# A decoder layer on one core: ones row by a transfer, group weights on VectorE, single scatters, bias halves moved

## The reference, cut to what matters

```python
x = _layernorm(x + _L0_attn_ref(x, ...), axis=-1)
x = _layernorm(x + _L0_xattn_ref(x, ctx_768, ...), axis=-1)
x = _layernorm(x + _L0_ffn_ref(x, ...), axis=-1)
```

```python
mean_sq = (jnp.sum(jnp.square(re), -1) + jnp.sum(jnp.square(im), -1)) / (2.0 * H * M)
rs = jax.lax.rsqrt(mean_sq[..., None] + 1e-05)
y = re * rs * norm_scale[:H * M] @ W_re + im * rs * norm_scale[H * M:] @ W_im
return y * x_gate @ out_proj_w
```

## Time and profile before

| | |
|---|---|
| median of 3 runs | 228.33 us (228.28 to 228.69) |
| profiled execution | 228.0 us, of it span 226.2 us |
| busy: PE, PEld | 183.7 (81%), 132.8 (59%) |
| busy: DVE, ACT, POOL | 160.5 (71%), 116.8 (52%), 71.4 (32%) |
| chain that ended last | PE 63%, DVE 22%, issue 4%, DMA 4%, ACT 4% |
| TensorE's mean granted clock | 0.93 |

### The profile page before, as it was taken

How to read it: one execution, slowest core, us unless ns; L and a number is a source line. 1 busy time by engine, 2 the same in 40 slices (tenths; PEclk the granted TensorE clock), 3 DMA queues, 4 the chain that set the end, 5 groups by cost and what they waited for, 6 DMA issues and landing times.

```text
span 226.2 us, 4759 instructions
## 1 busy us (share of the span) xinstructions
PE 183.7 (81%) x1727; PEld 132.8 (59%) x1727; DVE 160.5 (71%) x394; ACT 116.8 (52%) x245; POOL 71.4 (32%) x86
## 2 busy tenths in 40 slices
PE   7769999979799888999979739832799999998700
PEld 6434556654254646657636728632799999887500
DVE  2956999988899667477459625688466787754791
ACT  2056989722565225267937424544335676551353
POOL 8950000000030000025665286673015555451000
PEclk9979999999999999999979676995899999999985
DMA  5999999992996395989196013014221110003111
GB/s 151 294 197 251 190 260 204 382 407 105 244 380 158 85 317 182 244 295 280 64 293 219 7 41 113 12 34 107 60 63 49 38 35 26 19 3 109 36 42 41
DMA packets 13465, 34.15 MB, mean 151 GB/s; under 512 B 2095, under 2 KB 5733, under 8 KB 13442
## 3 DMA queue, kind: packets, MB, share of 16 engines
q1 hardware_dynamic: 12354, 32.22, 50.4%
q0 software_dynamic: 1088, 1.62, 2.4%
HBM read 27.96 MB, written 6.38 MB: 152 GB/s over the span
## 4 chain that ended last, share of the span: by engine, by line
PE 63%; DVE 22%; issue 4%; DMA 4%; ACT 4%; another core or an unknown queue 1%; POOL 0%; DVEq 0%; SPq 0%; ACTq 0%; POOLq 0%
PE bank L776 8%; PE bank L483 8%; PE bank L559 7%; PE bank L536 7%; PE bank L759 6%; PE bank L493 5%; PE bank L502 5%; PE bank L546 5%; PE bank L471 2%; PE bank L757 2%; DVE map_e L1421 2%; DVE neg_max L1341 2%; DVE dsm L1151 2%; DVE ph L1445 2%; DMA convw_sb<-conv_w 2%
## 5 line engine op out<-in xcount | busy, mean ns | idle before, releaser
L1588 DVE SCALAR_TENSOR_TENSOR ctx_slot<-bank,ctx_slot 128x512 f16<-128x512 f32 (+1 forms) x28 | 18.7, 672 | 15.2 <-ACT ctx_slot L1070 10.4
L1807 POOL DMA_INDIRECT ret<-ctx_slot,ctxT_slot x20 | 19.8, 989 | 30.2 <-ACT ctx_slot L1083 26.8
L536 PE MATMUL bank<-ctxT_slot,w_conv 97*64 97x500 f32 x96 | 23.5, 628 | 2.4 <-ACT pc L917 1.4
L1070 ACT ACTIVATE ctx_slot<-bank 128x512 f16<-128x512 f32 (+1 forms) x28 | 16.1, 582 | 15.8 <-PE bank L759 15.8
L483 PE MATMUL bank<-xpad,w_conv 128*128 128x448 f32 x48 | 20.3, 580 | 3.2 <-DVE w_conv L1142 3.2
L776 PE MATMUL bank<-home,ctx_slot 128*112 128x128 f16 (+1 forms) x192 | 14.7, 229 | 7.1 <-ACT ctx_slot L1070 7.1
L559 PE MATMUL bank<-ctx_slot,ph 125*64 125x96 f32 (+1 forms) x384 | 19.6, 265 | 0.4 <-DVE res L1451 0.4
L559 PEld LDWEIGHTS bank<-ctx_slot,ph 125*64 125x64 f32 (+1 forms) x384 | 18.1, 146 | 2.3 <-DVE res L1451 1.1
L483 PEld LDWEIGHTS bank<-xpad,w_conv 128*128 128x128 f32 x48 | 9.8, 206 | 13.3 <-issue 9.3
L776 PEld LDWEIGHTS bank<-home,ctx_slot 128*112 128x112 f16 (+1 forms) x192 | 12.8, 122 | 7.6 <-ACT ctx_slot L1070 7.4
L1341 DVE TENSOR_REDUCE neg_max<-bank 120x1 f32<-120x1500 f32 x8 | 13.7, 1717 | 4.3 <-PE bank L536 4.2
(11 more groups left out here) (220 smaller groups left out, 448.1 us busy)
## 6 DMA issues: line engine op xcount, KB each, us to landing
ctx_slot<-ctx SPq DMA_DIRECT2D x16, 576.0 KB, 5.5
ctxT_slot<-ctx_T SPq DMA_DIRECT2D x16, 562.5 KB, 8.7
w_raw<-w SPq DMA_DIRECT2D x16, 256.0 KB, 6.9
slots<-w_raw SPq DMA_DIRECT2D x4, 910.0 KB, 30.7
ctxT_slot<-slots SPq DMA_DIRECT2D x20, 65.0 KB, 1.9
convw_sb<-conv_w SPq DMA_DIRECT2D x3, 256.0 KB, 6.0
ctxT_slot<-ret SPq DMA_DIRECT2D x3, 224.0 KB, 3.3
small_sb<-small SPq DMA_DIRECT2D x1, 546.0 KB, 10.2
```

The source lines that it names most:

```text
L536: mm = pe.matmul(bank[j * GAP:j * GAP + rows, n, 0:SN], qk_all[:, at:at + rows], ctxT_slot[:, s, j, n * SN:(n + 1) * SN], start=True, stop ...
L1070: nc.scalar.activation(hh[:, n % 3, :, 0:cols], bank[:, n % 3, :].rearrange("p (f t) -> p f t", f=FC) [:, :, 0:cols], ACT.Relu).then_inc(t ...
L1588: V.scalar_tensor_tensor(hl[:, n % 3, :, 0:cols], bank[:, n % 3, :].rearrange("p (f t) -> p f t", f=FC) [:, :, 0:cols], 0.0, hh[:, n % 3, ...
L1807: G.indirect_dma_start(ret[:], bass.IndirectOffsetOnAxis(ap=xs_u[:, t, D + 1:D + 2], axis=0), out_st[:, t % OB, :], None, bounds_check=2 * ...
```

## The change

The ones row is no longer filled by POOL: a new input `ones`, one row of 9000 numbers, is transferred into it by SP behind the tokens and ahead of the context, and PE's wait at L706 is for that transfer. `w_blk` is made by DVE in two instructions, in the middle of `phases(0, 0)` and ahead of the clip; `norm_scale`, `w_ri` and a new table `group_of` (32 columns) stand in `first` for that. `scatter` takes one pair and one choice, so it is one instruction, and POOL's list places these between its other work; `split_low(1, 4)` comes ahead of three of them, and the last two splits and three `plus_beta` wait for `m_rw7`, the last pair's route weights. `bias_low` goes from turn 5 to the last turn, behind `select(3)`. Four more fillers stand on PE: one ahead of `logits(6)`, one ahead of `turn_x2(7)`, one ahead of `logits(7)`, and one ahead of `hidden(0)`.

```diff
@@ -73,8 +73,9 @@
 V_DOWN = 20
 
 
-FIRST = [("w_in", 3 * D), ("conv_b", 3), ("theta", M), ("slope", 1), ("dist", L), ("score_scale", 1), ("deriv", 3)]
-SMALL = [("norm_scale", 2 * M), ("w_ri", 2 * M * H), ("group_mask", D), ("ident", D), ("w_out", D), ("w_qT", D),
+FIRST = [("w_in", 3 * D), ("conv_b", 3), ("theta", M), ("slope", 1), ("dist", L), ("score_scale", 1), ("deriv", 3),
+         ("norm_scale", 2 * M), ("w_ri", 2 * M * H), ("group_of", K)]
+SMALL = [("group_mask", D), ("ident", D), ("w_out", D), ("w_qT", D),
          ("b_q", 1), ("w_k", DC + 1), ("w_v", D), ("w_r", E), ("b_r", E), ("gamma", D), ("beta", D), ("iota", E),
          ("dest", 2 * XP), ("region", E), ("extra", EXTRA)]
 HALF = [("before", PT), ("ident", 128), ("ones", TS), ("pick", E * TS)]
@@ -107,7 +108,7 @@
         self.eng.wait_ge(self.sem, value)
 
 
-def decoder_kernel(nc, x_T, x_tok, ctx, ctx_T, first, conv_w, small, half, bias, w_1, w_2, slots, ret, out):
+def decoder_kernel(nc, x_T, x_tok, ctx, ctx_T, first, conv_w, small, half, ones, bias, w_1, w_2, slots, ret, out):
     with ExitStack() as stack:
         def sb(name, shape, dt=F32):
             return stack.enter_context(nc.sbuf_tensor(name, shape, dt))
@@ -291,7 +292,7 @@
         s_cos = sem("cosines_done")
         s_sin = sem("sines_done")
         s_poly = sem("weighted_polynomial_done")
-        s_terms, s_rin = sem("products_ready"), sem("group_weights_scaled")
+        s_terms = sem("products_ready")
         s_re = sem("re_sums_done")
         s_ims = sem("im_sums_done")
         s_sq, s_fold = sem("squares_done"), sem("squares_folded")
@@ -393,6 +394,7 @@
             taps(GATE)
             sp_.dma_start(small_sb[:], small).then_inc(s_par, 16)
             sp_.dma_start(xtok[:], x_tok).then_inc(s_xtok, 16)
+            sp_.dma_start(ctxT_all[DC:DC + 1], ones).then_inc(s_ones, 16)
 
             def ctx_pair(i):
                 s = i % SLOTS
@@ -668,15 +670,16 @@
                 context_sum(PAIRS - 1)
                 ranks(3)
                 turn_x2(PAIRS - 2)
-                keep_warm(1, 0)
+                keep_warm(2, 0)
                 logits(PAIRS - 2)
                 turn_sum(PAIRS - 1)
                 keep_warm(1, 0)
                 values(PAIRS - 1)
                 ranks(4)
                 totals()
-                keep_warm(3, 0)
+                keep_warm(4, 0)
                 turn_x2(PAIRS - 1)
+                keep_warm(1, 0)
                 logits(PAIRS - 1)
 
 
@@ -703,7 +706,7 @@
             keep_warm(1, 0)
             query_keys(0)
             keep_warm(1, 0)
-            pe.wait_ge(s_ones, 1)
+            pe.wait_ge(s_ones, 16)
             scores(0)
             turn_x1(1)
             group_sums(1, 0, (1,))
@@ -1299,7 +1303,17 @@
                                           ALU.subtract, ALU.mult)
                 ins.then_inc(s_x1, 1)
 
-            phases(0, 0, between=lambda: clip(0))
+            def group_weights():
+                a = own.mark(V.tensor_tensor(w_rin[:], par("w_ri").rearrange("p (j h) -> p j h", j=2 * M),
+                                             par("norm_scale").unsqueeze(2).broadcast_to([128, 2 * M, H]), ALU.mult))
+                own.need(a)
+                V.tensor_tensor(w_blk[:].rearrange("p j (k h) -> p j k h", k=K),
+                                w_rin[:].unsqueeze(2).broadcast_to([128, 2 * M, K, H]),
+                                par("group_of").unsqueeze(1).unsqueeze(3).broadcast_to([128, 2 * M, K, H]), ALU.mult
+                                ).then_inc(s_blk, 1)
+                clip(0)
+
+            phases(0, 0, between=group_weights)
             phases(0, 1)
             polynomial(0)
             weights(0)
@@ -1528,8 +1542,6 @@
                 if i:
                     attended(i - 1, between=lambda: routed(i))
                 compared(i)
-                if i == 5:
-                    bias_low()
 
             def last_turn():
 
@@ -1541,6 +1553,7 @@
                 logit_read(PAIRS - 3, PAIRS - 2)
                 attended(PAIRS - 2, between=lambda: top_two(PAIRS - 3, PAIRS - 2))
                 select(3)
+                bias_low()
                 sum_copy(PAIRS - 1)
                 x2T_copy(PAIRS - 2)
                 place(3)
@@ -1710,18 +1723,6 @@
             G.memset(pattern[:, :, D + 1:].bitcast(U32), NOWHERE).then_inc(s_pat, 1)
             G.memset(b1_hl[:], 0.0)
             G.memset(b2_hl[:], 0.0).then_inc(s_bz, 1)
-            pool.wait_ge(s_bz, 1)
-            G.memset(ctxT_slot[DC:DC + 1], 1.0).then_inc(s_ones, 1)
-            pool.wait_ge(s_ones, 1)
-            pool.wait_ge(s_par, 16)
-            G.tensor_tensor(w_rin[:], par("w_ri").rearrange("p (j h) -> p j h", j=2 * M),
-                            par("norm_scale").unsqueeze(2).broadcast_to([128, 2 * M, H]), ALU.mult).then_inc(s_rin, 1)
-            pool.wait_ge(s_rin, 1)
-            for j in range(2 * M):
-                ins = G.tensor_tensor(w_blk[:, j, :].rearrange("p (k h) -> p k h", k=K),
-                                      w_rin[:, j, :].unsqueeze(1).broadcast_to([128, K, H]),
-                                      par("group_mask").rearrange("p (k h) -> p k h", k=K), ALU.mult)
-            ins.then_inc(s_blk, 1)
 
             def low_rows(i):
                 pool.wait_ge(r_hi, i + 1)
@@ -1743,17 +1744,15 @@
                 pool.wait_ge(r_exp, n + 1)
                 G.tensor_tensor(rows[:, w, 1, D], rows[:, w, 0, D], tsm[:, 1, w], ALU.mult).then_inc(r_wt, 1)
 
-            def scatter(n):
-
-                pairs = GROUPS[n]
+            def scatter(i, w):
+
+                n = [i in g for g in GROUPS].index(True)
                 pool.wait_ge(s_init, 16 * (E * REGION // PATTERN + 1))
-                pool.wait_ge(r_row, pairs[-1] + 1)
+                pool.wait_ge(r_row, i + 1)
                 pool.wait_ge(r_slot, n + 1)
                 pool.wait_ge(r_wt, n + 1)
-                for i in pairs:
-                    for w in range(2):
-                        G.indirect_dma_start(slots[:], bass.IndirectOffsetOnAxis(ap=slot_i[:, i, w:w + 1], axis=0),
-                                             rows[:, i, w, :], None).then_inc(r_scat, 16)
+                G.indirect_dma_start(slots[:], bass.IndirectOffsetOnAxis(ap=slot_i[:, i, w:w + 1], axis=0),
+                                     rows[:, i, w, :], None).then_inc(r_scat, 16)
 
             pool.wait_ge(s_sq, 4)
             G.tensor_tensor(sums[:, 0:2 * HW], sums[:, 0:2 * HW], sums[:, 2 * HW:4 * HW], ALU.add).then_inc(s_fold, 1)
@@ -1770,33 +1769,44 @@
             plus_beta(1)
 
             low_rows(2)
+            scatter(0, 0)
             split_low(0, 1)
-            scatter(0)
+            scatter(0, 1)
             split_low(1, 1)
+            scatter(1, 0)
             plus_beta(2)
 
             low_rows(3)
+            scatter(1, 1)
             split_low(0, 2)
             split_low(1, 2)
             second_weights(1)
             plus_beta(3)
 
             low_rows(4)
-            scatter(1)
+            scatter(2, 0)
             split_low(0, 3)
+            scatter(2, 1)
             split_low(1, 3)
+            scatter(3, 0)
             second_weights(2)
             plus_beta(4)
+            scatter(3, 1)
 
             low_rows(5)
-            scatter(2)
+            scatter(4, 0)
             second_weights(3)
             split_low(0, 4)
-            scatter(3)
+            scatter(4, 1)
+            split_low(1, 4)
+            scatter(5, 0)
             low_rows(6)
+            scatter(5, 1)
             second_weights(4)
-            scatter(4)
-            split_low(1, 4)
+            scatter(6, 0)
+            scatter(6, 1)
+
+            pool.wait_ge(m_rw7, 1)
             split_low(0, 5)
             split_low(1, 5)
             for i in range(PAIRS - 3, PAIRS):
@@ -1850,6 +1860,7 @@
         "deriv": rows(L0_attn_deriv_logits),
         "norm_scale": np.tile(ns, (K, 1)),
         "w_ri": np.tile(w_ri.reshape(H, 2 * M * H), (K, 1)),
+        "group_of": (group[:, None] == np.arange(K)[None]).astype(np.float32),
         "group_mask": (group[:, None] == group[None]).astype(np.float32),
         "ident": np.eye(128, dtype=np.float32),
         "w_out": f32(L0_attn_out_proj_w),
@@ -1886,6 +1897,7 @@
         "conv_w": cw.reshape(TAPS, 3, D).transpose(1, 0, 2).reshape(-1),
         "small": np.concatenate([small[name] for name, _ in SMALL], axis=1),
         "half": np.concatenate([half[name] for name, _ in HALF], axis=1).astype(np.float16),
+        "ones": np.ones((1, SLOTS * 2 * SK), np.float32),
         "bias": bias,
         "w_1": f32(L0_ffn_W1).transpose(0, 2, 1),
         "w_2": f32(L0_ffn_W2).reshape(E, D, FC, 128).transpose(0, 3, 2, 1).reshape(E, 128, FC * D),
```

## The result

The changed kernel takes 210.85 us in the median of four runs (208.87 to 213.15), beside 228.31 for the kernel before (227.07 to 228.69): a ratio of 0.9165, 95% interval 0.9104 to 0.9225. Forecast were 214.5, 209 to 221. The profiled execution took 208.87 (span 207.0, mean clock 0.97; before 228.0, 226.2 and 0.93), so it is a run at the quick end, and 19.2 us of span are to be accounted for. Lines of the new kernel are its own: `dsm` L1155 was L1151, PE's conv L485 was L483, `u_sb` L1453 was L1439, the x2T copy L1362 was L1348, the tile map's scaling L1435 was L1421.

A forecast was written before the change was run, and what follows sets the result against it. Bounds: DVE held by GpSimd at the start, at attention's end and behind it, with TensorE waiting or at low clock. 4.5 + 1.15 + 4.6 + 3.9 + 0.4 - 0.7 = 13.85 off 228.0; with the median's 0.33, 214.5; range 209 to 221.

The forecast's parts named there:

- Ones row: At the start: a transfer replaces GpSimd's fill, so DVE's scaling is no longer held; 4.8 less 0.3, so 4.5 us gained.
- Rival B: At the start: the gain meets something with a date of its own, DMA engines above all; 219 us, chance 0.11.
- Group weights: At the start: products moved to DVE take 1.3 us in its idle time, cost 0; larger first transfer costs 0.3.
- Bias halves: End of attention: DVE's maximum starts at 119.9 instead of 121.08, 1.15 us gained; cost 0 to 0.5 in the new place.
- Scatters: End of attention: placing scatters singly wins half of a possible 9.3 us, taken as 4.6, range 0 to 9.
- Rival A: End of attention: the scatters give nothing, since splits hold DVE as long as scatters do; 219.1 us, chance 0.2.
- Rival C: End of attention: all 9.3 us come back, clock included, and 1 more from the expert stage; 209 us, chance 0.12.
- the whole pot: End of attention: all that single scatters could win, 9.3 us from a long turn, late copies, a late read and low clock.
- The row at 134.76: End of attention: DVE's copy late by 1.16 us behind a split, taken as evidence that splits hold DVE too.
- Late wait: Behind attention: GpSimd waits for the last pair's weights, freeing DVE's tile map scaling; 3.9 us gained, between 3 and 4.6.
- Fillers: Four more TensorE fillers at 0.4 us each: two lie in waits, two stand ahead of ready work; 0.7 us lost.
- Tile stage: Tile stage and end: TensorE and DVE in a steady rhythm, to which the change adds nothing.

## Why the prediction was right, and where it was not

The direction, the range and the mechanism at the start were right; the time was 3.65 below the forecast, and the account of the profiled executions 5.35 above its sum of 13.85. Of these 5.35, 2.33 are the tile stage, at which no part of the change was aimed: that part of the gain was luck.

**Ones row.** Right in each step: scaling 0.23 (said: 0.15 to 0.3), no gap of TensorE, ACT's read at 13.26 (said: near 13.4), no wait for the new row. The stretch won 4.87 where 4.5 was said, since the larger first transfer did not cost its 0.3. Rival B (the lead runs into something with a date of its own) is out: the lead is 4.87 from the first maximum to the seventh, and putting the fill back costs 6.3.

**Group weights.** Right but for a tenth: 1.22 and 0.18 (1.3 was taken); the clip starts some 0.1 later for them, where 0 was said.

**Bias halves.** Sized too low: 1.15 was the old hold of 1.24, but the same pair in the new order is held for 2.87, and the part is worth 2.3 to 2.7. A price read off the old trace is that of an old coincidence.

**Scatters.** This is the step that failed, "I take half, 4.6", by its size and by its reason. The stretch won 7.39 where the terms made 5.05, and put back alone the bursts cost 8.2 to 9.5. The prediction weighed "scatters hold DVE" against "splits hold DVE just as much" and took the middle. Both can happen, and neither is the point: no held instruction of the 14 traces outlasts a pause of GpSimd of 0.08 or more, and it was pauses that the bursts lacked. Rival A (nothing won, 219.1), which rested on splits holding DVE too, had its fact right and its conclusion wrong. Rival C (the whole pot and clock, 209) comes nearest to the changed kernel's 208.9 to 213.2 and 208.0 to 212.5, with the help of the 2.33 of the tile stage, on which it had not counted. The row at 134.76 behind a split was the wrong witness: it is a copy out of PSUM, and the long holds of these traces are on instructions that read SBUF. The other late copies of the earlier trace rows, from which the pot took 3.7, were no safe sign of GpSimd's hand either, since ACT's copy was late beside the one at 113.58.

The Trainium skill, "SBUF — State Buffer", section "Who interferes with whom", has the shared port pair held "for the whole instruction", while the other engine "fully blocks". The traces agree on the block, and for the two holds of the tile map without the late wait (over at 141.67 and 142.77) on its length too. For others the length does not fit: by that rule the difference asked at 110.37 with bursts would have gone on at 110.83, after 0.46, and it took 4.87. The same section says that a VectorE instruction with two inputs from SBUF contends with GpSimd instructions that read SBUF; the held sums, products and differences quoted here are of this kind, the held scalings are not.

**Late wait.** 4.44 in that stretch where 3.9 was said, but the wait itself is worth only 1.5 there (2.2 to 3.4 in the total). In the changed order without the wait, the map met instructions of 1.10 and 0.78, not one of 4.72. What was queued behind it was not late for PE: PE's one long wait there, 1.89 at 146.66, is for DVE's own split (L1617), not for GpSimd's.

**Fillers.** The wrong sign: 0.7 lost was said, and without them the kernel is some 4 to 7 slower, by a way that the prediction did not have. Their own time does fall into waits: ACT's first read comes as early with them as without.

**Tile stage.** "The change adds nothing to them" was wrong by 2.33: the trace of before already had two rhythms in it, 1.73 us a tile and later 4.0 for two. The text called it steady without looking at its last third.

## What to carry to other kernels

When a tiny VectorE instruction lasts microseconds, look in GpSimd's timeline for the end of the unbroken run that it fell into, and not only for the end of the instruction beside it: the release can come at either. Break long runs of GpSimd work at the moments when VectorE needs SBUF twice: other work with a pause ahead of it will do, and so will a wait for the instruction just issued, which costs GpSimd about 0.1 us. And a stage that "runs steadily" deserves a table of its last third: it can have two rhythms, and a few fillers ahead of it can make one of them likelier, by a way that isn't clear yet.

## What the runs showed of the hardware that was not expected

- A held VectorE instruction can stay held over several GpSimd instructions: 4.87, 4.88 and 4.67 us in runs of five to six, none of them over 1.2. None outlasts GpSimd's next pause of 0.08 us or more. But over twenty holds of the 14 traces end earlier, where one GpSimd instruction ends and the next follows without a pause (141.67 and 142.77 above; `sel` at 95.75 in the changed kernel, over at 96.28 between two `low_rows`), and three end about 0.3 ahead of the pause, within the run's last addition. What decides which boundary frees it is open. A hold can start under a scatter (110.37, 129.58 and 132.17 above), whose own length is 0.94, but most instructions that start there run free.
- The late copies out of PSUM in the kernel before are not explained: the bursts did not bring them back, and ACT's copy at 114.36 was 1.37 late beside them.
- One tile stage, with equal instructions and a clock of 1.00, runs at 1.73 us a tile or at 2.0 to 2.2, and once at the second it stays there.
